# Attention stage of a GNN kernel: second MLP layer in a first-layer bank, next Q rows behind the strip sums, chunk sums between halves, one-hot rows for Q on ScalarE

## What is computed

```python
def _L0_gnn_ref(h, efeat, src, dst, Wq, Wk, Wv, W1, b1, W2, b2, Wo, bo):
    Q = (h @ Wq).reshape(n, H, HD)          # 8 heads of 32
    K = (h @ Wk).reshape(n, H, HD)
    V = (h @ Wv).reshape(n, H, HD)
    score = jnp.einsum('ehd,ehd->eh', Q[dst], K[src]) / np.sqrt(HD)
    score = score + jax.nn.relu(efeat @ W1 + b1) @ W2 + b2
    m = jax.ops.segment_max(score, dst, num_segments=n)
    ex = jnp.exp(score - m[dst])
    denom = jax.ops.segment_sum(ex, dst, num_segments=n)
    alpha = ex / denom[dst]
    out = jax.ops.segment_sum(alpha[:, :, None] * V[src], dst, num_segments=n)
    return out.reshape(n, D) @ Wo + bo
```

## Time and profile before

| | us |
|---|---|
| median of 3 runs | 3524.32 |
| fastest, slowest | 3522.18, 3537.6 |
| profiled execution, its own time | 3527.64 |
| its span | 3525.7 |
| attention stage in it | about 113 to 1033 |

### The profile page before, as it was taken

One profiled execution on the slowest core, in us unless ns is written; L12 is line 12 of the kernel. 1 busy time (PEld: TensorE's weight loads), 2 busy tenths in 40 slices (PEclk: granted clock), 3 DMA queues, 4 the chain that ended last, 5 costly groups with the idle time before them and its releaser, 6 DMA issues.

```text
span 3525.7 us, 64349 instructions
## 1 busy us (share of the span) xinstructions
PE 2560.2 (73%) x18318; PEld 1985.6 (56%) x18422; DVE 1970.7 (56%) x6179; ACT 682.7 (19%) x1571; POOL 1737.9 (49%) x1779
## 2 busy tenths in 40 slices
PE   7566767666765565556767676577777699999997
PEld 6344334434435555554555555456665478888775
DVE  3477777676756555556667676667767621111222
ACT  3223333333330000001111111011111231111110
POOL 0554444444407777776777776677777500000000
PEclk9788887787766878787889888798889889999998
DMA  5876555565503333333333343333333322332221
GB/s 187 246 208 175 173 173 170 164 179 166 170 20 101 109 110 111 109 110 95 114 120 115 117 123 97 91 116 115 118 112 113 97 79 98 103 102 93 88 96 58
DMA packets 185480, 435.80 MB, mean 124 GB/s; under 512 B 42835, under 2 KB 89161, under 8 KB 185417
## 3 DMA queue, kind: packets, MB, share of 16 engines
q0 software_dynamic: 93184, 272.74, 26.7%
q1 hardware_dynamic: 88634, 159.04, 13.9%
q10 hardware_dynamic: 3600, 3.28, 0.3%
HBM read 390.37 MB, written 44.51 MB: 123 GB/s over the span
## 4 chain that ended last, share of the span: by engine, by line
PE 31%; POOL 26%; issue 21%; DVE 13%; DMA 6%; ACT 2%; SPq 1%; DVEq 1%; POOLq 0%; ACTq 0%
POOL gath L767 25%; PE banks L1411 15%; DVE prod L1752 3%; PE banks L1256 3%; DMA gath<-h_table,idx_slot 3%; PE banks L1239 2%; PE banks L1170 2%; DVE rh L1756 2%; DVE gath L1780 2%; DVE rh L1780 2%; PE banks L1303 1%; PE banks L1227 1%; DMA misc<-counts 1%; PE banks L1080 1%; PE banks L1242 1%
## 5 line engine op out<-in xcount | busy, mean ns | idle before, releaser
L767 POOL DMA_INDIRECT gath<-h_table,idx_slot x1248 | 1293.2, 1036 | 371.3 <-issue 344.5
L1256 PE MATMUL banks<-onehot,gath 128*128 128x128 f32 x4992 | 782.6, 323 | 479.8 <-DMA gath<-h_table,idx_slot 451.6
L1256 PEld LDWEIGHTS banks<-onehot,gath 128*128 128x128 f32 x4992 | 730.8, 233 | 538.0 <-DMA gath<-h_table,idx_slot 452.2
L1411 PE MATMUL banks<-gath,misc 128*128 128x256 bf16 x1875 | 516.5, 275 | 0.0
L1411 PE MATMUL banks<-acc,misc 128*128 128x256 bf16 x2500 | 421.4, 277 | 23.4 <-DMA misc<-counts 14.5
L765 POOL DMA_INDIRECT rh<-kv_table,idx_slot x208 | 211.1, 1015 | 215.3 <-PE banks L1230 163.1
L765 POOL DMA_INDIRECT gath<-kv_table,idx_slot x208 | 209.0, 1005 | 214.0 <-PE banks L1230 159.7
L1314 PE MATMUL banks<-gath 128*128 128x512 bf16 x624 | 243.7, 414 | 64.7 <-DVE gath L1958 64.7
L1411 PEld LDWEIGHTS banks<-acc,misc 128*128 128x128 bf16 x2500 | 243.4, 99 | 70.3 <-issue 16.8
L1958 DVE TENSOR_SCALAR gath<-w_qkv 128x800 bf16<-128x800 f16 x728 | 257.5, 424 | 0.0
L1838 DVE TENSOR_TENSOR acc<-acc,banks 128x256 f32 x156 | 65.3, 418 | 339.0 <-PE banks L1256 327.2
(11 more groups left out here) (217 smaller groups left out, 3552.4 us busy)
## 6 DMA issues: line engine op xcount, KB each, us to landing
misc<-counts SPq DMA_DIRECT2D x75, 800.0 KB, 4.3
counts<-misc SPq DMA_DIRECT2D x26, 800.0 KB, 3.9
gath<-h_table,idx_slot POOLq DMA_INDIRECT x1248
rh<-in_dst_rows SPq DMA_DIRECT2D x106, 128.0 KB
w_qkv<-in_ef_t SPq DMA_DIRECT2D x106, 128.0 KB
q_win<-q_table SPq DMA_DIRECT2D x208, 64.0 KB
rh<-mask_dram SPq DMA_DIRECT2D x424, 8.0 KB
kv_table<-onehot SPq DMA_DIRECT2D x25, 256.0 KB, 2.0
```

What stands on the lines that cost most here:

```text
L767: pool.indirect_dma_start(row_slot[:, k, t, :], None, source, row_index).then_inc(gath_done[k][t // HALF], 16)
L1256: last = nc.tensor.matmul(banks[:, 3 * k + c, 0:P], row_slot[:, k, t, c * P:(c + 1) * P], onehot[:, k, t, :], start=(t == 0), stop=(t == T ...
L1411: last = nc.tensor.matmul(banks[:, slot, 0:D], c_slot[:, slot, c, :], parts[n % 2][j][:, c, :], start=(c == 0 and j == 0), stop=(c == NB - ...
```

## The change

Second layer: `mlp_scores` writes the lower half of bank 2 (`HID_BANK`) instead of bank 4, no longer waits for `s_ready` (`scores_back` does), and `hidden` of the next group waits for `s_copied`. `mlp_scores` now comes ahead of `turn_scores`. Q rows of half 0 of the next group (`q_rows(g + 1, 0)`) stand behind the second `tile_sums`, in the body before; `turn_weights(g)` moves into body g. `add_chunk` handles chunk g-2 in body g, between the two halves on DVE, and the block steps follow it. The one-hot rows are made by ACT as relu(1 - |node - dst|). An exponential on a single column (`warm`) loads the exponential's table ahead of `finish_rows`.

```diff
...
 LOW, UP = slice(0, D), slice(D, 2 * D)
 B_ROWS, B_TURN = 6, 7
-MLP_BANK, S_BANK, SUM_BANK, WIN_BANK = 4, 5, 6, 7
+HID_BANK, MLP_BANK, S_BANK, SUM_BANK, WIN_BANK = 2, 4, 5, 6, 7
 EX_AT, EX_END, DEN_ROWS = 3 * P, 3 * P + TG * HEADS, D
...
                 sp.dma_start(mask[t * HEADS:(t + 1) * HEADS, k, 0:SPAN + 1], mask_dram[:, bass.ds(at, SPAN + 1)].partition_broadcast(HEADS)
                              ).then_inc(mask_in[k], 16)
-        def load_q(g):
-
-            for half in range(2):
+        def load_q(g, halves):
+
+            for half in halves:
                 first = sp.value_load(half_i[0:1, bass.ds(g * 2 + half, 1)], min_val=0, max_val=NA - QW)
                 wait(sp, q_done, g * 2 + (half - 1))
                 for r in range(2):
...
         def prefetch(g, k, i, b):
             if isinstance(g, int) and g == NG:
                 load_mask(g, k % 2)
+                load_q(g, (0,))
             if isinstance(g, int) and g >= NG:
                 return
             load_ef(g + 1, (k + 1) % 2, i)
             load_mask(g, k % 2)
-            load_q(g)
+            load_q(g, (0, 1))
             load_dst(g + 1)
         each_four(sp, prefetch)
...
                 nc.scalar.activation(std[:, :], mv[:, 1:2], ACT.Sqrt, bias=eps[:, :]).then_inc(g_std, 1)
     def windows_path():
+        def make_oht(g):
+
+            act.wait_ge(dst_in, g * 32 + 32)
+            wait(act, q_done, g * 2)
+            for half in range(2):
+                last = nc.scalar.activation(oht[:, half, :], dst_row[:, half, :], ACT.Abs, scale=-1.0,
+                                            bias=half_node[:, bass.ds(g * 2 + half, 1)])
+            last.then_inc(oht_far, 1)
+            act.wait_ge(oht_far, g + 1)
+            nc.scalar.activation(oht[:, :, :], oht[:, :, :], ACT.Relu, scale=-1.0, bias=one[:, :]).then_inc(oht_ready, 1)
+
         def relu(g, u):
             c, half = u // 2, u % 2
             act.wait_ge(hid_done, g * 4 + (u + 1))
             wait(act, mlp_done, g)
-            nc.scalar.activation(hid[:, u, :], banks[:, 2 + half, :], ACT.Relu, bias=b1c[:, c:c + 1]).then_inc(hid_evac, 1)
+            nc.scalar.activation(hid[:, u, :], banks[:, HID_BANK + half, :], ACT.Relu, bias=b1c[:, c:c + 1]).then_inc(hid_evac, 1)
         def mlp_copy(g, k):
             act.wait_ge(mlp_done, g + 1)
             wait(act, s_back, g - 1)
-            nc.scalar.activation(s_heads[:, k, :], banks[:, MLP_BANK, LOW], ACT.Identity, bias=b2c[:, :]).then_inc(s_copied, 1)
+            nc.scalar.activation(s_heads[:, k, :], banks[:, HID_BANK, LOW], ACT.Identity, bias=b2c[:, :]).then_inc(s_copied, 1)
         def exponent(c):
             act.wait_ge(shifted, c + 1)
...
         for r in range(4):
             if r == 0:
                 act.wait_ge(qkv_free, NB + 3)
+                act.wait_ge(setup_done, 1)
+                make_oht(0)
             relu(0, r)
         mlp_copy(0, 0)
...
             c, kc = g - 1, (k + 1) % 2
             if not isinstance(g, int) or g:
                 weights_copy(c, kc)
+            if full:
+                relu(g + 1, 0)
+                relu(g + 1, 1)
             if not isinstance(b, int) or b > 0:
                 if k % 2 == 0:
                     roots(PASS_VALUE, b - 1)
-            if full:
-                relu(g + 1, 0)
-                relu(g + 1, 1)
             if blocks and k % 2 == 1:
                 turn_block(PASS_VALUE, b)
-            if not isinstance(b, int) or b > 0:
-                if k % 2 == 0:
-                    finish_rows(PASS_VALUE, b - 1)
             if full:
                 relu(g + 1, 2)
                 relu(g + 1, 3)
+            if not isinstance(b, int) or b > 0:
+                if k % 2 == 0:
+                    nc.scalar.activation(warm[:, :], eps[:, :], ACT.Exp)
+                    finish_rows(PASS_VALUE, b - 1)
+            if full:
+                mlp_copy(g + 1, kc)
+                make_oht(g + 1)
             if blocks and k % 2 == 0:
                 stage_block(PASS_VALUE, b)
             if not isinstance(g, int) or g:
                 sums_copy(c)
-            if full:
-                mlp_copy(g + 1, kc)
             if not isinstance(g, int) or g < CHUNKS:
                 exponent(g)
...
             if c == 0:
                 pe.wait_ge(ef_done[k], loads * 32)
+                wait(pe, s_copied, g)
             for half in range(2):
                 wait(pe, hid_evac, g * 4 + (c * 2 + half - 1))
-                nc.tensor.matmul(banks[:, 2 + half, :], w1[half * FE:(half + 1) * FE, c * P:(c + 1) * P],
+                nc.tensor.matmul(banks[:, HID_BANK + half, :], w1[half * FE:(half + 1) * FE, c * P:(c + 1) * P],
                                  ef[half * FE:(half + 1) * FE, k, :], start=True, stop=True).then_inc(hid_done, 1)
         def mlp_scores(g):
             pe.wait_ge(hid_evac, g * 4 + 4)
-            wait(pe, s_ready, g)
             for c in range(FC):
                 for j in range(4):
-                    last = nc.tensor.matmul(banks[j * STRIP:(j + 1) * STRIP, MLP_BANK, LOW], w2_wide[:, c, :],
+                    last = nc.tensor.matmul(banks[j * STRIP:(j + 1) * STRIP, HID_BANK, LOW], w2_wide[:, c, :],
                                             hid[:, c * 2 + j // 2, j % 2 * QUARTER:(j % 2 + 1) * QUARTER],
                                             start=(c == 0), stop=(c == FC - 1))
             last.then_inc(mlp_done, 1)
...
         def scores_back(g, k):
             pe.wait_ge(s_copied, g + 1)
+            wait(pe, s_ready, g)
             for h in range(2):
                 last = nc.tensor.transpose(banks[:, MLP_BANK, UP].rearrange("p (j q r) -> p q j r", j=4, q=2)[:, h, :, :],
                                            s_heads[:, k, h * P:(h + 1) * P], ident[:, :])
...
             hidden(0, 0, 1, c)
         mlp_scores(0)
         scores_back(0, 0)
+        q_rows(0, 0)
         def fused(g, k, i, b):
             full = not isinstance(g, int) or g < NG
...
             blocks = not isinstance(b, int) or b >= 0
             kc, kn = (k - 1) % RING, (k + 1) % 2
             loads = (g + 1) // 2 + 1 if isinstance(g, int) else i * 2 + ((k + 1) // 2 + 1)
-            if value:
-                turn_weights(g - 1)
             if full:
-                q_rows(g, 0)
                 hidden(g + 1, kn, loads, 0)
                 q_rows(g, 1)
+                hidden(g + 1, kn, loads, 1)
             if blocks and k % 2 == 1:
                 wait(pe, chunk_added, g - 1)
                 turn_back(PASS_VALUE, b)
-            if full:
-                hidden(g + 1, kn, loads, 1)
             if value:
                 if blocks and k % 2 == 1:
                     pe.wait_ge(rows_done, b + 1)
...
                 elif blocks:
                     wait(pe, var_done, b)
                 tile_sums(g - 1, kc, 0)
-                tile_sums(g - 1, kc, 1)
+            if full:
+                mlp_scores(g + 1)
             if not isinstance(g, int) or g < CHUNKS:
                 turn_scores(g, k, i)
+            if value:
+                tile_sums(g - 1, kc, 1)
             if full:
-                mlp_scores(g + 1)
+                q_rows(g + 1, 0)
                 scores_back(g + 1, kn)
+            if not isinstance(g, int) or g < CHUNKS:
+                turn_weights(g)
             if value:
                 window_sums(g - 1, kc)
             if blocks and k % 2 == 0:
...
     dve.wait_ge(loaded, 16 * N_LOADS)
     nc.vector.memset(zero_b[:, :], 0.0)
     nc.vector.memset(eps[:, :], EPS)
+    nc.vector.memset(one[:, :], 1.0)
     nc.vector.memset(xcol[:, :, :, HEADS:HEADS + 1], 1.0)
     nc.vector.tensor_copy(part_f[:, :], part_i[:, :])
     link(nc.vector.tensor_copy(iota_f[:, :], iota_i[:, :]))
...
             last.then_inc(oh_ready, 1)
-        def make_oht(g):
-
-            dve.wait_ge(dst_in, g * 32 + 32)
-            wait(dve, q_done, g * 2)
-            for half in range(2):
-                last = V.tensor_scalar(oht[:, half, :], dst_row[:, half, :], half_node[:, bass.ds(g * 2 + half, 1)], None, ALU.is_equal)
-            last.then_inc(oht_ready, 1)
-
         def half_scores(g, k, i, half):
             dve.wait_ge(ring_in[k][half], i * (8 * TG) + 8 * TG)
...
             last.then_inc(oh_strip, 1)
         dve.wait_ge(b2_loaded, 32)
-        make_oht(0)
         chain_at, size = chain_total(chain), LINKS[PASS_VALUE]
         def fused(g, k, i, b):
...
             c, kc = g - 1, (k - 1) % RING
             before = not static or b > 0
             if blocks and k % 2 == 0:
-                chain.enter(b * size + (chain_at - 4) if before else chain_at)
+                chain.enter(b * size + (chain_at + 4 - size) if before else chain_at)
             if full:
                 half_scores(g, k, i, 0)
+            if not static or g > 1:
+                add_chunk(g - 2)
             if before and k % 2 == 0:
-                norm_apply(PASS_VALUE, b - 1)
+                norm_stats(PASS_VALUE, b - 1)
```

(20 more changed lines are left out.)

3 lines of the change are left out of this document (added).

## The result

| | before | changed |
|---|---|---|
| median, us | 3524.89 (4 runs) | 3351.44 (4 runs) |
| fastest, slowest | 3522.18, 3537.6 | 3344.58, 3366.51 |
| ratio to before | | 0.9507 (0.9465 to 0.9549) |
| ratio, a second series of 6 runs | | 0.9554 (0.9523 to 0.9584), median 3361.56 |
| profiled execution, its span | 3527.64, 3525.7 | 3344.58, 3342.7 |

The change is faster by 4.5 to 5%: 173 us at the medians, where 142 were forecast. The forecast time of 3383 us is 32 us too high.

A forecast was written before the change was run, and what follows sets the result against it. Bound: a chain in series through DVE, PE and ACT in the attention loop, no engine full. Saving (17.97 - 14.9) x 41 = 126 us plus 16 in ten early groups, together 142, giving 3383 us; range 3330 to 3455.

The forecast's parts named there:

- the turn's chain: Attention loop, one end of window sums to the next: even body 16.3 us, odd 12.6, a pair 28.9.
- the period: Attention loop, time per group by the last instruction of `shift_scores`: 17.97 us before, 14.9 forecast.

## What to carry to other kernels

In a loop over several in-order engines, count the turn's chain with what stands behind each moved step in every other queue: one step moved by one place on TensorE was worth 3.8 us of 18, and 0.5 us less work on the busiest engine nothing. Where a clock can fall, read all turns before taking one as typical: here alike turns took 14.4 and 17.0 us. Look at the granted clock in the gaps of TensorE: if it falls there, a few useless matmuls in a wait are the cheapest trial, and they tell how much of a wait is clock. When a period is taken from first and last rows, count the intervals.

## What the chip showed that I had not expected

Useless matmuls raised the granted clock from 0.80 to 1.00 over 640 us and took 13% off the period (17.54 to 15.25), with DMA share up from 0.55 to 0.63. And a delay is amplified: 0.6 us on the path over ScalarE gave 1.1 per group, with a lower clock (0.89 for 0.93). That the clock makes the difference is argued from this row, not shown apart.
